# State-space layer: the work between two batches' scans in another order, Softplus as one function, and v of two head pairs at once

## The chip, the cores and the metric

One Trainium2 chip, one of its NeuronCores. The metric is the device time in microseconds (us) from the start of the kernel to its end. TensorE (PE), VectorE (DVE), ScalarE (ACT), GpSimd (POOL) and the DMA queue of SyncE (SP) each run their own list of instructions in order; they wait for each other only through semaphores.

## What is computed

Four transformer-like layers on x of shape 8 x 512 x 256 (batches, positions, features), fp32. Layers 0 and 2 are attention with 16 heads of 16 features, layer 1 is attention with 16 heads of 64 (pairs of heads share 128 columns), layer 3 is a bidirectional state-space (Mamba) layer with a gated MLP. Only layers 1 and 3 are touched. Layer 3, cut to what matters:

```python
def _mamba(h, ...):
    xz = h @ in_proj_W                      # 256 -> 2 x 512
    x, z = jnp.split(xz, 2, axis=-1)
    x = _silu(causal_conv4(x) + conv_b)     # 4 taps
    xdbl = x @ x_proj_W                     # 16 + 32 + 32 columns
    dt = softplus(xdbl[..., :16] @ dt_proj_W + dt_proj_b)
    Bm, Cm = xdbl[..., 16:48], xdbl[..., 48:]
    A = -jnp.exp(A_log)
    def step(hst, inp):                     # over 512 positions
        dA = jnp.exp(dt_t[:, :, None] * A)
        hst = hst * dA + dt_t[:, :, None] * B_t[:, None, :] * x_t[:, :, None]
        y = jnp.einsum('bdn,bn->bd', hst, C_t)
        return (hst, y)
    y = scan(step) + Dp * x
    return y * _silu(z) @ out_proj_W
h = modulate(_ln(x)); fwd = _mamba(h); bwd = flip(_mamba(flip(h)))
x = x + g1 * (fwd + bwd)
h = modulate(_ln(x)); x = x + g2 * (_silu(h @ w1) * (h @ w2) @ w3)
```

In layer 1 the part that matters is `v = h @ Wv` of each head.

## The kernel before

The layers run one after the other; each keeps its weights in SBUF and loops over the 8 batches, with an all-engine barrier after each batch. Nothing is scheduled by a compiler: every engine's list is the order in which the functions below issue instructions.

**Layer 1** (`wide_attention_layer`). `project(pair, which, to)` makes q, k or v of one pair of heads in one PSUM bank, `projected` copies it out on ACT. v is made as 4 position tiles x 2 contraction chunks of matmuls with 128 moving columns (L1016), one v per pair; `values` multiplies the probabilities with it.

**Layer 3** (`mamba_layer`). A batch has two parts.

*The scans.* 2 directions x 16 groups of two states x 4 chunks of 128 channels make 128 units (`UNITS`). For unit i ACT makes two `decay` halves (Exp, L1869) and its share of `dtx_B` (dt·x times B, L1860; 7 instructions for every 4 units on ACT and 1 on POOL, L1797), PE transposes dtx_B into one of two pairs of PSUM banks (`fill_bx`, L1897), DVE runs the recurrence over 2 x 512 positions in one instruction (`scan_unit`, L1827), POOL multiplies the state by C (L1812, tile `hc`) and PE sums it over the states (`y_sum`, L1908). There are three decay buffers, three of h, four of hc. The last `y_sum` of a chunk is added and gated on DVE (`combine_last`, L1837 and L1840).

*Between the scans* (`between_*`). The end of batch b and the start of batch b + 1 are woven together: LayerNorm of the next batch (stats and scaling on DVE, L90 to L101; reciprocal root on POOL, L107 and L110; transposes on PE, L117; scale and shift on ACT into `hT`, L125), input projection in 8 chunks of 128 (`project_in`, L1650; x in the first four, z in the others), `out_proj` of batch b (L1661), the gate rows (L191, L198, L204), 24 convolution taps on DVE (L1530, the first tap on ACT, L1575), Silu (L1591, L1584), x_proj (L1674), dt_proj (L1684), transposes of B (L1697), Softplus, residual and second LayerNorm of batch b, the MLP (L1713, L1634, L1561, L1738), dt·x and its transposes (L1556, L1727, L1624). Softplus is built as max(v, 0) + ln(1 + exp(-|v|)): Abs (L1604), max on DVE (L1543), Exp (L1615), Ln (L1619), an addition on DVE (L1553). SP copies dt to 128 partitions (`dt_rep`, 16 DMAs, L1492) and C to DRAM (L1487), and waits for all of them at the end (L1495). Then comes the barrier, and after it the first 7 scalings `dtx_B`, the first decays and the first fill, before the first scan can start.

Before batch 0 the start half runs alone, after batch 7 the end half alone.

## Time and profile before

| | us |
|---|---|
| median of 3 runs | 6822.93 (6816.15 to 6824.26) |
| the profiled execution | 6823.96 |
| its span, first to last instruction | 6822.1 |
| PE busy | 6011.6 (88%) |
| DVE busy | 4556.8 (67%) |
| ACT busy | 4284.6 (63%) |
| POOL busy | 2641.1 (39%) |

The state-space layer starts at 3662 us and takes the rest, 3160 us. In it one batch repeats every 387.55 us. Times below are on the span's clock. In the rows, a line "start us, us, engine line op" is a run of like instructions; brackets at its end give the idle time before it and what ended it.

### The profile page before, as it was taken

To read this page: it belongs to the slowest core of one execution; us is meant where nothing else is said; L and a number is where in the kernel's file an instruction comes from. 1 tells how busy PE (TensorE), PEld (TensorE's weight loads), DVE (VectorE), ACT (ScalarE), POOL (GpSimd) and SP (SyncE) were. 2 spreads that over 40 slices of the span, in tenths; PEclk is the share of its full clock that TensorE was granted. 3 is DMA by queue.
4 is the path that set the end of the run, shared out by engine and by line. 5 is a ranking of instruction groups with operands and counts; after the bars stand their busy time and mean duration, and the time that the engine had idled before them with its cause. 6 is when DMAs were issued, how large, how long until landed. Compare 5 with 4: busy or idle time off the path is not lost. (4 is left out here: it accounts for less than half of the span.)

```text
span 6822.1 us, 79092 instructions
## 1 busy us (share of the span) xinstructions
PE 6011.6 (88%) x29136; PEld 3143.3 (46%) x29136; DVE 4556.8 (67%) x5015; ACT 4284.6 (63%) x6948; POOL 2641.1 (39%) x1956
## 2 busy tenths in 40 slices
PE   6989987999999996998986898888898888888898
PEld 3444444555555553453443444444444444444444
DVE  4565743344344434566573997979798897979797
ACT  2344434444454542434443988979797998979796
POOL 0000002222222220000000876949495785949496
PEclk8999998999999997999997998989899998989899
DMA  4312211000000002131221101011100201010100
GB/s 108 54 31 52 33 29 39 1 1 1 1 1 1 1 1 53 30 58 32 52 37 41 34 19 52 27 44 30 41 30 15 56 21 51 29 43 29 41 30 19
DMA packets 152081, 216.13 MB, mean 32 GB/s; under 512 B 23649, under 2 KB 90489, under 8 KB 151185
## 3 DMA queue, kind: packets, MB, share of 16 engines
q1 hardware_dynamic: 151552, 211.01, 13.7%
q8 instruction: 233, 3.82, 0.2%
q14 instruction: 152, 1.24, 0.1%
q10 hardware_dynamic: 144, 0.07, 0.0%
HBM read 146.48 MB, written 30.44 MB: 26 GB/s over the span
## 5 line engine op out<-in xcount | busy, mean ns | idle before, releaser
L1827 DVE TENSOR_TENSOR_SCAN l__h<-l__decay,l__psum 128x1024 f32<-128x1024 f32 x1024 | 2278.0, 2272 | 113.0 <-ACT l__decay L1869 90.3
L1812 POOL TENSOR_TENSOR l__hc<-l__h,l__c_rep 128x1024 f32<-128x1024 f32 x1024 | 2039.8, 2003 | 220.6 <-DVE l__h L1827 176.6
L1897 PEld LDWEIGHTS l__psum<-ident,l__dtx_B 128*128 128x128 f32 x8192 | 900.2, 143 | 1151.0 <-DVE l__h L1827 653.4
L1897 PE MATMUL l__psum<-ident,l__dtx_B 128*128 128x128 f32 x8192 | 1142.3, 284 | 305.8 <-ACT l__dtx_B L1860 258.1
L1869 ACT ACTIVATE l__decay<-l__dt_rep,l__a_neg 128x511 f32<-128x511 f32 x2048 | 1355.2, 714 | 2.5 <-DVE l__h L1827 2.4
L1860 ACT ACTIVATE l__dtx_B<-l__dtx_T,l__b_T 128x512 f32<-128x512 f32 x1792 | 1199.7, 715 | 71.9 <-PEq L1922 60.7
L1908 PE MATMUL l__psum<-l__hc,l__gather 128*64 128x512 f32 x4096 | 1111.9, 621 | 18.3 <-POOL l__hc L1812 17.9
L107 POOL TENSOR_SCALAR l__ln_var_eps<-l__ln_mean_var 128x4 f32<-128x4 f32 x64 | 15.2, 237 | 2424.9 <-DVE l__ln_mean_var L93 2424.3
L566 DVE TENSOR_REDUCE l__row_max<-l__psum 128x1 f32<-128x512 f32 x1024 | 657.4, 686 | 249.4 <-PE l__psum L581 248.1
L1055 POOL TENSOR_SCALAR l__probs<-l__probs,l__rec 128x512 f32<-128x512 f32 x512 | 349.5, 696 | 968.4 <-DVE l__rec L1051 968.4
L759 ACT ACTIVATE l__probs<-l__psum 128x1024 f32<-128x1024 f32 x512 | 515.7, 1025 | 282.6 <-PE l__psum L808 278.1
L1041 DVE TENSOR_REDUCE l__neg_max<-l__psum 128x2 f32<-128x1024 f32 x256 | 312.9, 1223 | 437.1 <-PE l__psum L1035 436.3
L581 PE MATMUL l__psum<-l__k_stack,l__q_stack 96*128 96x512 bf16 (+1 forms) x1024 | 418.9, 422 | 137.7 <-PEq L931 87.6
L1181 ACT ACTIVATE l__probs_T<-l__psum 128x512 f32<-128x512 f32 x256 | 152.8, 597 | 446.9 <-PE l__psum L1219 446.9
L1046 ACT ACTIVATE l__probs<-l__psum,l__neg_max 128x512 f32<-128x512 f32 x512 | 346.7, 682 | 44.6 <-DVE l__neg_max L1041 27.1
L808 PE MATMUL l__psum<-l__q_stack,l__k_stack 98*128 98x512 bf16 (+1 forms) x1024 | 333.7, 417 | 8.7 <-ACT l__probs L759 4.4
L1035 PE MATMUL l__psum<-l__kT,l__qT 64*128 64x512 f32 x1024 | 296.3, 656 | 35.4 <-PEq L1324 24.0
L1219 PEld LDWEIGHTS l__psum<-ident,l__probs 128*128 128x128 f32 x2048 | 224.6, 143 | 203.3 <-POOL l__probs L1055 121.0
L1908 PEld LDWEIGHTS l__psum<-l__hc,l__gather 128*64 128x64 f32 x4096 | 203.5, 135 | 207.9 <-issue 168.5
L581 PEld LDWEIGHTS l__psum<-l__k_stack,l__q_stack 96*128 96x128 bf16 (+1 forms) x1024 | 98.8, 98 | 435.1 <-DVE l__row_max L566 291.3
L917 PE MATMUL l__psum<-l__w,l__g 128*128 128x256 f32 x1024 | 278.1, 380 | 12.4 <-ACT l__g L781 12.4
L1219 PE MATMUL l__psum<-ident,l__probs 128*128 128x128 f32 x2048 | 288.4, 284 | 0.6
(169 smaller groups left out, 7042.8 us busy)
## 6 DMA issues: line engine op xcount, KB each, us to landing
l__c_rep<-l__c_dram SPq DMA_DIRECT2D x512, 128.0 KB, 2.8
l__dt_rep<-l__dt SPq DMA_DIRECT2D x128, 256.0 KB, 4.9
l__parts_dram<-l__parts SPq DMA_DIRECT2D x64, 384.0 KB, 4.5
l__q_stack<-l__parts_dram SPq DMA_DIRECT2D x192, 128.0 KB, 6.6
l__k_stack<-l__parts_dram SPq DMA_DIRECT2D x192, 128.0 KB, 9.7
l__w<-in_l_w SPq DMA_DIRECT2D x6, 1024.0 KB, 9.1
mod_w<-in_mod_w SPq DMA_DIRECT2D x2, 2816.0 KB, 12.8
x_sb<-in_x SPq DMA_DIRECT2D x1, 4096.0 KB, 27.4
```

The source lines that it names most:

```text
L566: nc.vector.tensor_reduce(mx[:, h // GH, t, h % GH:h % GH + 1], max_bank(n), AX.X, ALU.max).then_inc(S["max_taken"], 1)
L581: nc.tensor.matmul(max_bank(n), qs[0:k_max, h, t * P:(t + 1) * P], ks[0:k_max, h, :], start=True, stop=True).then_inc(S["max_filled"], 1)
L759: nc.scalar.activation(probs[:, n % SLOTS:n % SLOTS + 2, :], pair(n), ACT.Exp, scale=float(HD) ** -0.5).then_inc(S["exp"], 1)
L1046: nc.scalar.activation(probs[:, u % SLOTS, j, :], bank[QK + 2 * (u % 2) + j], ACT.Exp, bias=neg_max[:, u % SLOTS, j:j + 1], accum_out=sums ...
L1055: nc.gpsimd.tensor_scalar(probs[:, u % SLOTS, j, :], probs[:, u % SLOTS, j, :], rec[:, u % SLOTS, j:j + 1], 1.0, ALU.mult, ALU.mult)\
L1219: last = nc.tensor.transpose(bank[TR + j][:, k * P:(k + 1) * P], probs[:, u % SLOTS, j, k * P:(k + 1) * P], ident[:, :])
L1812: nc.gpsimd.tensor_tensor(hc[:, i % HCS, :, :], h[:, i % HS, :, :], c_of_i, ALU.mult).then_inc(S["hc"], 1)
L1827: nc.vector.tensor_tensor_scan(both(h[:, i % HS, :, :]), both(decay[:, i % DECAYS, :, :]), both(bx_psum(i)), 0.0, ALU.mult, ALU.add).then_ ...
L1860: nc.scalar.activation(dtx_B[:, k % 2, t, :, j, :], dtx_T[:, w, t, :].rearrange("p (b d) -> p b d", d=HB), ACT.Copy, scale=b_T[:, w, t, NJ ...
L1869: nc.scalar.activation(decay[:, i % DECAYS, s, 1:T], dt_rep[:, w, c, s, 1:T], ACT.Exp, scale=a_neg[:, g, c, s:s + 1]).then_inc(S["decay"], 1)
L1897: last = nc.tensor.transpose(bx_psum(i)[:, s, t * P:(t + 1) * P], dtx_B[:, k % 2, t, 2 * c + s, :, :].rearrange("p j d -> p (j d)"), ident ...
L1908: last = nc.tensor.matmul(y_psum[half(s), c, :], gather[:, :], hc[:, i % HCS, s, :], start=(g == 0), stop=(g == GROUPS - 1))
```

## The change

1. Layer 1: v is made for two pairs of heads at once. The PSUM bank that took four position tiles of one pair takes two position tiles of two pairs: 2 tiles x 2 chunks of matmuls with 256 moving columns instead of 4 x 2 with 128. The number of ACT copies stays.
2. Softplus is one ACT function (ACT.Softplus), straight from PSUM; Abs, Exp, Ln, the max and the addition go.
3. The next batch's LayerNorm statistics are taken on DVE after unit 123 of 128, its scaling after unit 125; PE transposes them after unit 126's scan. The four first `project_in` stand around the last `y_sum` in PE's list. ACT's `hT` waits for all 128 hc.
4. dt_proj, B and C of the two directions lie in different rows: direction 0 has dt in rows 0 to 31 and B in 64 to 95, direction 1 has dt in rows 64 to 95 and B in 32 to 63. x_proj goes to banks 6 and 7, and its first chunk stands between two `project_in`.
5. The 7 first scalings on ACT and the one on POOL, the first two decays and the first two fills are issued ahead of the barrier; the scans' waits count from there. dt_rep has a semaphore per chunk, and SP waits only for C at the end.
6. Tiles that live only between the scans are laid out around the new early buffers with gaps; `decay` and `c_rep` swap places.

The core of the diff:

```diff
 (project, layer 1)
-                for t in range(TT):
+                both = slice(pair // 2 * 2 * P, (pair // 2 + 1) * 2 * P)
+                for u in range(2):
+                    t = pair % 2 * 2 + u
                     for c in range(DC):
-                        last = nc.tensor.matmul(to[:, t * P:(t + 1) * P], hT[:, c, t * P:(t + 1) * P], wv[:, c, cols],
+                        last = nc.tensor.matmul(to[:, u * 2 * P:(u + 1) * 2 * P], hT[:, c, t * P:(t + 1) * P],
+                                                wv[:, c, both], start=(c == 0), stop=(c == DC - 1))
 (mamba_layer)
+    FILLED = 2
+    DECAYED = DECAYS - 1
+    STATS_AFTER, SCALED_AFTER = UNITS - 5, UNITS - 3
+    dt_rows = (slice(0, DTL), slice(2 * NS, 2 * NS + DTL))
+    c_rows = (slice(DTL, DTL + NS), slice(0, NS))
+    b_rows = (slice(DTL + NS, DTL + 2 * NS), slice(NS, 2 * NS))
 (between_gpsimd)
+            if begin:
+                pool.wait_ge(S["taps"], 2 * (TAPS - 1) * IC)
+                nc.gpsimd.memset(decay[:, :, :, 0:1], 0.0).then_inc(S["zero"], 1)
+                pool.wait_ge(S["bT"], 1)
+                pool.wait_ge(S["dtxT"], 2 * IC)
...
+                scale_last(0)
 (between_vector)
-            if begin:
-                ahead.stats(nc, dve, nxt, 0)
-            if end:
-                combine_last(0)
-            if begin:
-                ahead.scaled(nc, dve, nxt, 0)
             if end:
-                for c in range(1, IC):
+                for c in range(IC):
                     combine_last(c)
...
-                    nc.vector.tensor_scalar(relu(c), dt_banks(c), dtb[:, c:c + 1], 0.0,
-                                            ALU.add, ALU.max).then_inc(S["relu"], 1)
...
-                    nc.vector.tensor_tensor(dt_all[:, c, :, :], relu(c), dt_all[:, c, :, :], ALU.add).then_inc(S["dt"], 1)
 (between_scalar)
+            def softplus(c):
+                act.wait_ge(S["dt_filled"], c + 1)
+                nc.scalar.activation(dt_all[:, c, :, :], dt_banks(c), ACT.Softplus, bias=dtb[:, c:c + 1])\
+                    .then_inc(S["dt"], 1)
...
+                act.wait_ge(S["c_out"], 32)
+                act.wait_ge(S["dtxT"], 2 * IC)
+                for q in range(IC):
+                    scale_pair(q)
...
+                for i in range(DECAYED):
+                    act.wait_ge(s_dt_rep[split(i)[2]], dt_rep_of(nxt))
+                    decay_unit(i)
 (between_tensor)
+                if c == 3:
+                    pe.wait_ge(S["dt"], 1)
+                for w in range(2):
+                    last = nc.tensor.matmul(dt_banks(c)[:, w, :], dtw[dt_rows[w], c * P:(c + 1) * P],
+                                            dc[dt_rows[w], w, :], start=True, stop=True)
...
+                for i in range(FILLED):
+                    fill_bx(i)
 (the scans, DVE)
+                        if i == STATS_AFTER and begin:
+                            ahead.stats(nc, dve, b + 1, 0)
+                        if i == SCALED_AFTER and begin:
+                            ahead.scaled(nc, dve, b + 1, 0)
 (the scans, ACT)
+                    act.wait_ge(S["hc"], UNITS)
+                    between_scalar(act, True, begin, b + 1)
 (the scans, PE)
+                    if begin:
+                        pe.wait_ge(S["scan"], UNITS - 1)
+                        norm.tensor(nc, pe, 0, bank[0:DC])
                     y_sum(UNITS - 2)
+                    if begin:
+                        pe.wait_ge(S["scan"], UNITS)
+                        pe.wait_ge(S["hT"], DC)
+                        project_in(pe, 0)
+                        project_in(pe, 1)
                     y_sum(UNITS - 1)
+                    if begin:
+                        project_in(pe, 2)
+                        project_in(pe, 3)
```

How the lists stand, in two places. PE at the end of a batch's scans and through the gap, first before (L1908 is y_sum, L1650 the input projection, L1661 the output projection, L1674 x_proj, L1684 dt_proj, L1713 the MLP's first matmuls, L1727 the transposes of dt·x):

```order
L1908 MATMUL l__psum<-l__hc,l__gather 64x512 x8
L117 MATMUL l__psum<-ident,l__ln_xn 128x128 x8
L1650 MATMUL l__psum<-l__hT,l__win 128x512 x8
L1661 MATMUL l__psum<-l__wout,l__silu_z 128x256 x16
L198 MATMUL l__psum<-l__gate_diag,ones 128x256 x2
L1650 MATMUL l__psum<-l__hT,l__win 128x512 x8
L1674 MATMUL l__psum<-l__xs,l__xproj 96x512 x8
L1684 MATMUL l__psum<-l__dt_and_c,l__dtw 128x512 x4
L1697 MATMUL l__psum<-ident,l__dt_and_c 128x32 x8
L1684 MATMUL l__psum<-l__dt_and_c,l__dtw 128x512 x4
```

and now PE at the same place (L1975 is y_sum, L1710 the input projection, L1719 the output projection, L1731 x_proj):

```order
L1975 MATMUL l__psum<-l__hc,l__gather 64x512 x4
L117 MATMUL l__psum<-ident,l__ln_xn 128x128 x8
L1975 MATMUL l__psum<-l__hc,l__gather 64x512 x2
L1710 MATMUL l__psum<-l__hT,l__win 128x512 x4
L1975 MATMUL l__psum<-l__hc,l__gather 64x512 x2
L1710 MATMUL l__psum<-l__hT,l__win 128x512 x4
L1719 MATMUL l__psum<-l__wout,l__silu_z 128x256 x16
L198 MATMUL l__psum<-l__gate_diag,ones 128x256 x2
L1710 MATMUL l__psum<-l__hT,l__win 128x512 x4
L1731 MATMUL l__psum<-l__xs,l__xproj 96x512 x2
L1710 MATMUL l__psum<-l__hT,l__win 128x512 x4
L1731 MATMUL l__psum<-l__xs,l__xproj 96x512 x6
```

The last y_sum, unit 127's, now stands behind two chunks of the input projection; before, all sums stood ahead of it.

ACT from x_proj's result to the next batch's scans, before (L1594 takes it from PSUM, L1860 are the scalings, L1869 the decays; the two branches are the barrier):

```order
L1594 ACTIVATE l__dt_and_c<-l__psum 96x512 x2
L1599 ACTIVATE l__y<-l__xs,l__dp 128x512 x4
L1604 ACTIVATE l__dt<-l__psum,l__dtb 128x1024 x2
L1608 ACTIVATE l__b_T<-l__psum 128x256
L1604 ACTIVATE l__dt<-l__psum,l__dtb 128x1024 x2
L125 ACTIVATE l__hT_mlp<-l__psum,l__cur 128x512 x2
L1615 ACT_TABLE_LOAD
L1615 ACTIVATE l__dt<-l__dt 128x1024 x4
L1619 ACT_TABLE_LOAD
L1619 ACTIVATE l__dt<-l__dt 128x1024 x4
L1624 ACTIVATE l__dtx_T<-l__psum 128x4x128 x4
L1634 ACT_TABLE_LOAD
```

and now (L1677 takes x_proj's result, L1649 is Softplus, L1661 the MLP's Silu, L1505 the scalings, L1520 the decays; rows up to the barrier):

```order
L1677 ACTIVATE l__dt_and_c<-l__psum 96x512 x2
L1649 ACT_TABLE_LOAD
L1649 ACTIVATE l__dt<-l__psum,l__dtb 128x1024 x2
L1681 ACTIVATE l__b_T<-l__psum 128x256
L1649 ACTIVATE l__dt<-l__psum,l__dtb 128x1024 x2
L125 ACTIVATE l__hT_mlp<-l__psum,l__cur 128x512 x2
L1655 ACTIVATE l__dtx_T<-l__psum 128x4x128 x2
L1661 ACT_TABLE_LOAD
L1661 ACTIVATE l__hid<-l__psum 128x512
L1655 ACTIVATE l__dtx_T<-l__psum 128x4x128 x6
L1505 ACTIVATE l__dtx_B<-l__dtx_T,l__b_T 128x8x64 x7
L1661 ACTIVATE l__hid<-l__psum 128x512 x2
```

Behind them an ACT_TABLE_LOAD and four decays (L1520) stand ahead of the barrier too. Five table loads a batch become four; the four instructions of y_first (L1599 before) stand ahead of x_proj's result.

## Rows read from the trace of the kernel before

**Rows 1.** The profile page, part 1: busy time and share of the span by engine.

```profile
PE 6011.6 (88%) x29136; PEld 3143.3 (46%) x29136; DVE 4556.8 (67%) x5015; ACT 4284.6 (63%) x6948; POOL 2641.1 (39%) x1956
```

**Rows 2.** Stretches: length, then busy us (instructions) by engine, granted clock, DMA.

```profile
4065.80:4071.00 5.20, 5.20 (x8) 2.39 (x9) 1.78 (x6) 1.28 (x2) 0.00 (x0) 0.62 0.00 0
...
4101.00:4112.70 11.70, 10.86 (x19) 4.26 (x17) 5.36 (x5) 5.45 (x7) 0.00 (x0) 0.50 0.00 0
...
4151.10:4446.00 294.90, 264.34 (x1521) 135.18 (x1519) 287.70 (x137) 288.44 (x471) 272.73 (x158) 0.99 0.09 28
```

**Rows 3.** Timeline, batch 0's last scans and the restart behind the barrier.

```profile
4046.45 11.00 DVE L1827 TENSOR_TENSOR_SCAN l__h<-l__decay,l__psum 128x1024 f32<-128x1024 f32 x5 [0.16 <-ACT l__decay L1869]
...
4057.60 2.00 POOL L1812 TENSOR_TENSOR l__hc<-l__h,l__c_rep 128x1024 f32<-128x1024 f32 x1 [0.18 <-DVE l__h L1827]
...
4143.94 4.39 ACT L1860 ACTIVATE l__dtx_B<-l__dtx_T,l__b_T 128x512 f32<-128x512 f32 x7 [9.21 <-PEq L1922]
...
4148.35 1.28 ACT L1869 ACT_TABLE_LOAD   x1
...
4151.11 4.46 DVE L1827 TENSOR_TENSOR_SCAN l__h<-l__decay,l__psum 128x1024 f32<-128x1024 f32 x2 [6.98 <-ACT l__decay L1869]
```

**Rows 4.** Timeline, the gap's first 14 us: next LayerNorm, projection, first tap.

```profile
4057.43 1.40 DVE L90 BATCH_NORM_STATS2 l__ln_stats<-x_sb 128x6 f32<-128x256 f32 x4
...
4058.86 0.38 DVE L93 BATCH_NORM_AGGREGATE l__ln_mean_var<-l__ln_stats 128x2 f32<-128x6 f32 x4
...
4060.00 1.43 POOL L110 TENSOR_TENSOR l__ln_rstd<-l__ln_var_eps,minus_half 128x4 f32<-128x4 f32 x1
...
4061.47 1.38 DVE L101 TENSOR_SCALAR l__ln_xn<-x_sb,l__ln_mean_var,l__ln_rstd 128x256 f32<-128x256 f32 x4 [0.93 <-POOL l__ln_rstd L110]
...
4064.21 1.54 ACT L125 ACTIVATE l__hT<-l__psum,l__cur_ahead 128x512 f32<-128x512 f32 x2 [11.92 <-PE l__psum L117]
...
4069.69 0.60 ACT L1571 ACTIVATE l__x_padded<-l__psum 128x512 f32<-128x512 f32 x1 [3.94 <-PE l__psum L1650]
...
4071.24 15.99 DVE L1530 SCALAR_TENSOR_TENSOR l__xs<-l__x_padded,l__conv_w,l__xs 128x512 f32<-128x512 f32 x24 [3.62 <-ACT l__xs L1575]
```

**Rows 5.** Timeline, x_proj to the last Abs of Softplus.

```profile
4090.19 7.11 PE L1674 MATMUL l__psum<-l__xs,l__xproj 128*96 128x512 f32 x16 [0.69 <-ACT l__silu_z L1584]
...
4097.34 0.59 ACT L1594 ACTIVATE l__dt_and_c<-l__psum 96x512 f32<-96x512 f32 x1 [0.27 <-PE l__psum L1674]
4097.83 2.54 ACT L1599 ACTIVATE l__y<-l__xs,l__dp 128x512 f32<-128x512 f32 x4
...
4099.81 0.61 PE L1697 MATMUL l__psum<-ident,l__dt_and_c 32*128 32x32 f32 x7
...
4110.05 1.11 ACT L1604 ACTIVATE l__dt<-l__psum,l__dtb 128x1024 f32<-128x1024 f32 x1 [2.30 <-PE l__psum L1684]
```

**Rows 6.** Timeline, MLP, Ln and the end of the gap.

```profile
4112.78 12.90 PE L1713 MATMUL l__psum<-l__hT_mlp,l__w 128*128 128x512 f32 x24 [0.87 <-ACT l__hT_mlp L125]
...
4119.24 3.90 ACT L1619 ACTIVATE l__dt<-l__dt 128x1024 f32<-128x1024 f32 x4
...
4133.90 7.37 PE L1738 MATMUL l__psum<-l__w,l__hid 128*128 128x256 f32 x24
...
4142.03 0.69 DVE L222 TENSOR_TENSOR x_sb<-x_sb,l__res_tmp 128x512 f32<-128x512 f32 x1
```

**Rows 7.** Timeline, the same MLP matmuls behind batch 7.

```profile
6810.72 5.45 PE L1738 MATMUL l__psum<-l__w,l__hid 128*128 128x256 f32 x24 [1.41 <-DVE l__hid L1561]
```

**Rows 8.** Timeline, the start half alone: dt's copies, and ACT behind the barrier.

```profile
3734.88 16.20 SPq L1492 DMA_DIRECT2D l__dt_rep<-l__dt  x16
...
3756.39 4.39 ACT L1860 ACTIVATE l__dtx_B<-l__dtx_T,l__b_T 128x512 f32<-128x512 f32 x7 [11.25 <-PEq L1766]
```

**Rows 9.** Timeline, PE in layer 1: one v projection and what follows it.

```profile
1243.73 1.95 PE L1016 MATMUL l__psum<-l__wv,l__hT 128*128 128x128 f32 x16
1245.52 1.04 PE L117 MATMUL l__psum<-ident,l__ln_xn 128*128 128x128 f32 x8
```

More of the change, by code:

```diff
@@ L1027, in projected @@
             else:
[L1028 removed]
+                half = slice(pair % 2 * 2, pair % 2 * 2 + 2)
+                nc.scalar.activation(v[:, pair // 2 % 2, half, :].rearrange("p t n -> p (t n)"), of, ACT.Copy)\
                     .then_inc(S["proj"], 1)
@@ new lines, in silu_x, with y_first @@
+            def silu_x(c):
+                for w in range(2):
+                    act.wait_ge(S["taps"], 2 * ((TAPS - 1) * c + TAPS - 2) + w + 1)
+                    nc.scalar.activation(xs[:, c, w, :], xs[:, c, w, :], ACT.Silu).then_inc(S["xs"], 1)
+            def y_first(c):
+                act.wait_ge(S["xs"], 2 * (c + 1))
+                if end:
+                    act.wait_ge(S["gated"], c + 1)
+                nc.scalar.activation(y[:, c, :], xs[:, c, 0, :], ACT.Copy,
+                                     scale=dp[:, c:c + 1]).then_inc(S["y_first"], 1)
@@ L1628, in between_scalar @@
+            if end:
+                norm.scalar(nc, act, 1 if begin else 0, bank[6:8], hT_mlp, cur, scale2, shift2)
             if begin:
                 take_dtx_T(0)
-                take_dtx_T(1)
             if end:
-                for j in range(HC):
-                    act.wait_ge(S["up_filled"], j + 1)
-                    nc.scalar.activation(hid[:, j, :], bank[UP_BANKS[j][0]], ACT.Silu).then_inc(S["silu"], 1)
+                silu_up(0)
             if begin:
-                take_dtx_T(2)
@@ L1864, in decay_unit, with decays @@
[L1864 to L1865 removed]
+                            act.wait_ge(S["bx_filled"], IC * (k - 1) - FILLED)
+                        scale_pair(q)
+                    def decays(i):
                         if i >= DECAYS:
                             act.wait_ge(S["scan"], i - DECAYS + 1)
[L1868 to L1870 removed]
```

427 lines of the change are left out of this document (224 added, 203 removed).

## The prediction

> **What bounds the kernel now.** I read the page's busy times first [rows 1]: PE is busy 88% of the span, which says nothing on the state-space layer, where one batch repeats every 387.55 us (ACT's first scaling at 3756.39 and at 4143.94) [rows 3, 8]. So I cut one batch into two stretches and read each.
>
> In the **scans** (4151.1 to 4446.0) ACT is busy 288.44 of 294.90 us, DVE 287.70, PE 264.34 at clock 0.99 [rows 2]. ACT sets the pace: up to unit 123 DVE still waits for a decay, and from there it runs five scans in 11.00 us, 2.20 each, on its own [rows 3]. ACT issued 225 scalings and 248 decay halves, 473 instructions, and one table load (1.28) between the barrier at 3756.39 and scan 123 at 4046.45: 290.06 us, so (290.06 - 1.28) / 473 = 0.6105 us each [rows 3, 8]. DVE alone would have needed about 124 x 2.20 + 3 = 276.
>
> In the **gap** nothing is full. Take t = 0 at the end of the last scan, 4046.45 + 11.00 = 4057.45 [rows 3]. Then: hT ready at 8.3, input projection from there at clock 0.62, first tap of DVE at 13.8, taps done at 29.8 [rows 2, 4]; x_proj 32.7 to 39.9, its result out at 40.5, last Abs done at 53.7 with PE at clock 0.50, Ln from 61.8 to 65.7, MLP's last matmul 83.8, last residual 85.3, barrier released 86.5, first scan 93.7 [rows 2, 3, 5, 6]. It is a chain from engine to engine, and the sum is a new chain.
>
> **The scans, part by part.** Seven scalings, one load and four decay halves leave the stretch behind the barrier: 11 x 0.6105 + 1.28 = 8.0 us less, since ACT sets the pace from barrier to unit 123. Their cover in the gap: between the transposes of dt·x and the MLP's second and third Silu, ACT waits for PE anyway (below). The statistics and the scaling of the next batch enter DVE's list after unit 123 and 125, where DVE is alone on the path: 0.15 (copy) + 1.40 + 0.38, less overlaps, 1.85, plus 1.38 [rows 4] = 3.3 us more. POOL's root (1.43, [rows 4]) has two scans of time, 4.4 us, beside one product of 2.0: no wait. Net -4.7 us for batches 0 to 6, -8.0 for batch 7, which has no next one: 7 x 4.7 + 8.0 = **-40.9**.
>
> **The gap's head.** Now LayerNorm's chain (8.3 us) is gone, but hT waits for the last product hc: POOL works 4057.60 to 4059.60 [rows 3], so hT starts at 2.25 and takes 1.54 [rows 4]: 3.8. PE then starts the input projection, 4.5 us earlier than before. This is not what DVE gets. The sum of unit 127 stands behind two chunks of the projection, and `combine_last(3)` and the gate diagonals stand ahead of the taps on DVE. From hT to the first chunk before was 3.95 us (4065.75 to 4069.69, [rows 4]; low clock, [rows 2]), the second chunk 1.7 more, the sum 1.1: 3.8 + 5.65 + 1.15 = 10.6. Then 1.33 for the combination and 0.9 for the gates: taps from 13.0, against 13.8 before. Without that wait they could start at 3.8 + 3.95 + 1.55 = 9.3. So of 4.5 us the path keeps 0.8, and the gap's head as a whole costs 3.3 in the scans for it. Taps 15.99: done at **29.0**.
>
> **x_proj and dt.** Silu of z and x alternate, and three quarters of x_proj no longer wait for all of z. Output projection from 14.0 (32 matmuls of 256 columns, 6.9 by 5.45 / 24 less the tail, [rows 7]), gates 1.0, gate rows 22.6, table load to 23.9; then 0.55 a Silu (0.60 for the like copy, [rows 4], less its overlap with the next); the fourth chunk's input projection pair ends at 30.4, silu of chunk 2 at 32.1, three y_first (2.54 / 4 = 0.63 each, [rows 5]) at 34.0, silu of chunk 3 at 35.1. Last x_proj pieces 35.15 to 36.9, second copy out 37.7 (before 40.5): 2.8 us won, against 3.6 had y_first(0..2) not stood ahead. Softplus' table load runs to 39.0 while PE makes dt.
>
> dt_proj of the two directions lies in row strips 0 and 64. The trace has the like: transposes out of rows 64 to 95 start at 4099.81, in the middle of dt_proj out of rows 0 to 31, which runs on to 4110 [rows 5]. I take it that the strips overlap, so four matmuls take three slots, then two per step. Slots are 0.43 at the high clock; in this stretch the clock was 0.50 from about 3 us after its start [rows 2], and then they are 0.85. dt ready at 39.4, 40.2, 43.9, 45.6 (one by one, as before, the last would be at 37.7 + 12.1 = 49.8). I price Softplus like Abs, Exp and Ln of the same 1024 columns, 1.11 alone and 3.90 for four [rows 5, 6]: done at 40.5, 41.5, 45.0, 46.7. The trace shows no Softplus; the lower bound is that row, the upper is open and is the rival below.
>
> By the Trainium skill, "TensorE: Matmul & The Clock Gate", Part 3: matmuls in different row groups run at the same time; by that rule the forecast stands, against it the serial rival. By "ScalarE activation tables: per-element evaluation and per-set limits", section "What a function is on this engine", the price of an ACTIVATE does not depend on the function and a change of set costs 1283 ns; the table loads agree (1.28), no run yet shows Softplus.
>
> **MLP and end.** LayerNorm 2 is long ready (xn at 36.4). Its transposes 47.0, hT_mlp 48.3, first transposes of dt·x 48.6, first up projection at low clock (0.85 a matmul for the first 5 us, which is how 24 of them took 12.90 before instead of 10.5, [rows 6]) to 54.4. Then three rounds of transposes and copies, 1.4 each, to 59.2; ACT's seven scalings, 4.39, to 63.6, while PE makes the other two up projections, 58.3 to 65.2. Silu and product 66.7. Down projection: 5.45 where PE had idled 1.4 us and stayed at the high clock [rows 7], 7.37 where it had not [rows 6]; 5.3 here, to 72.0. Residual 73.5; the two early fills on PE to 73.9 (now the last work, 1.9 us, 3.7 at low clock); barrier 1.2 [rows 3, 6]: release at **75.2**, with ACT's load and four decays done at 70. dt's copies: first issue 40.5, the eighth by 48.6, and 5.3 us to land (3751.08 to 3756.4, [rows 8]): 54, before ACT needs them at 67. Against 86.5: -11.3 a gap, x 7 = **-79.1**.
>
> **The start half alone.** Before, dt's first copy went at 3734.88, the last 16.2 later, and the barrier waited for it: 3756.39 [rows 8]. Now: taps end 3704.9, x_proj out 3708.7, Softplus 3711.6 to 3716.9, transposes 3720.8, scalings 3725.2, load 1.28, decays 2.56, barrier 1.2: 3730.3, so **-26**.
>
> **Small terms.** v in layer 1: 16 matmuls of 128 columns take 1245.52 - 1243.73 = 1.79 us [rows 9]; 8 of 256 take 5.45 / 24 x 8 = 1.82 by the MLP's row with its tail, 1.71 without [rows 7]: up to 0.08 x 64 = **-5**, between 0 and -8 where PE is not what is waited for. The layer's weights: two more DMAs behind a memset of the whole x_proj tile: **+1.5**.
>
> **Sum:** -40.9 - 79.1 - 26 - 5 + 1.5 = -149.5, from 6823.96 (this execution; the median is 6822.93): 6674. I say **6674 us**.
>
> **Rivals.**
> *The clock stays high.* x_proj, dt and the up projection follow more closely; if 0.85 never appears, dt comes 2 us earlier, the first up projection 2.6: release at 70.5, 7 x 4.7 = 33 us less: 6641. Against it: PE fell to 0.50 in just this work of 32 rows [rows 2].
> *Row strips don't overlap.* dt's last 4.2 us later, in 8 places: +34, 6708. With the fills at low clock (+1.8 x 7) 6720.
> *Softplus is dear (the other side).* Four a batch stand on the path, 8 batches. They cancel the gain at 149.5 / 32 = 4.7 us more each, 5.8 in all; at 7 us each the time is 6674 + 32 x 5.9 = 6863. For it: no row has the function. Against it: all four functions in the rows cost the same.
> *It doesn't do what it says.* If the barrier still waited for something, it would be dt's copies: their last lands at 41 + 16.2 + 5.3 = 62, before 75. So no.
>
> **How the numbers follow.** Forecast (6650 to 6700) 0.58; clock high (below 6650) 0.17; strips serial or more low clock (6700 to 6730) 0.17; worse but faster still 0.05; Softplus dear, or the scans slowed, beyond 6838: 0.03. A gap's release is uncertain by 3 us, 21 in all, the scans by 0.5 a batch. The range 6630 to 6722 leaves out 0.2. Faster by over 0.2% (14 us, about what a measurement tells from no change) 0.96, within 0.01, slower 0.03.
>
> **What would show it.** Batch period 371.5 us: last scan 296.4 behind the barrier, release 75 behind it. DVE idle from about 4 to 10.7 us in the gap, ended by y_sum; first tap at 13.0; Softplus 1.1 us each; first scan within 0.1 us of the barrier. Wrong if Softplus is longer, if the scans' period is no longer 15 ACT instructions in 9.16 us, or if fills or copies end the gap later than 77.

## The result, and the profile of the changed kernel

The changed kernel takes **6622.64 us** (median of 4 runs, 6619.90 to 6629.14) where the kernel before takes 6819.68 (4 runs): ratio 0.9713, 95% interval 0.9700 to 0.9725. The forecast was 6674, with a range of 6630 to 6722. The direction was right, the size too small by some 50 us: the time lies below the range.

The profiled execution of the changed kernel took 6629.14 us, its span 6627.4. First the page's busy times (they answer to [rows 1]). Then two rows of the changed kernel that cut the span: the first weight DMA of the state-space layer, and the group of all 1024 scans of DVE (shortest, median and longest ns, then the start of the first and of the last). The pair behind them is the same from the kernel before.

```profile
PE 5888.8 (89%) x28624; PEld 3055.1 (46%) x28624; DVE 4491.2 (68%) x4951; ACT 4212.2 (64%) x6876; POOL 2643.4 (40%) x1956
```

```profile
3642.19 0.41 SPq L1466 DMA_DIRECT2D l__win<-in_l_win  x1
...
L1904 DVE TENSOR_TENSOR_SCAN l__h<-l__decay,l__psum x1024: 2251/2261/2290, 3714.8 to 6571.4; 128x1024 f32<-128x1024 f32 x171
```

```profile
3662.56 0.41 SPq L1453 DMA_DIRECT2D l__win<-in_l_win  x1
...
L1827 DVE TENSOR_TENSOR_SCAN l__h<-l__decay,l__psum x1024: 2258/2262/2290, 3763.6 to 6767.2; 128x1024 f32<-128x1024 f32 x171
```

Cut there, the 194.7 us between the spans fall apart as follows. The forecast is put into the same cuts: the 7.2 us between barrier and first scan [rows 3] count to the start, so -26 + 1.5 - 7.1 there.

| stretch | before | changed | difference | forecast |
|---|---|---|---|---|
| layers 0 to 2 | 3662.56 | 3642.19 | -20.4 | -5 |
| layer 3 up to the first scan | 101.0 | 72.6 | -28.4 | -31.6 |
| first scan to last scan | 3003.6 | 2856.6 | -147.0 | -112.9 |
| last scan to the end | 54.9 | 56.0 | +1.1 | 0 |

Two terms carry the miss: the batches (34 us) and the layers ahead (15 us). The batches first. This is the gap behind batch 0 in the changed kernel, from its timeline (start, length, engine, line, operation, what ended the idle time before); t = 0 is the end of the last scan, 4007.96 + 4.45 = 4012.41. It answers to [rows 3 to 6].

```profile
4007.96 4.45 DVE L1904 TENSOR_TENSOR_SCAN l__h<-l__decay,l__psum 128x1024 f32<-128x1024 f32 x2
4012.55 2.00 POOL L1888 TENSOR_TENSOR l__hc<-l__h,l__c_rep 128x1024 f32<-128x1024 f32 x1 [0.18 <-DVE l__h L1904]
4014.64 1.45 ACT L125 ACTIVATE l__hT<-l__psum,l__cur_ahead 128x512 f32<-128x512 f32 x2 [10.37 <-POOL l__hc L1888]
4016.23 6.56 PE L1710 MATMUL l__psum<-l__hT,l__win 128*128 128x512 f32 x8 [1.83 <-ACT l__hT L125]
4022.72 1.08 PE L1975 MATMUL l__psum<-l__hc,l__gather 128*64 128x512 f32 x4
4023.85 0.69 DVE L1914 TENSOR_TENSOR l__y<-l__psum,l__y 128x512 f32<-128x512 f32 x1 [6.09 <-PE l__psum L1975]
4050.37 0.59 ACT L1677 ACTIVATE l__dt_and_c<-l__psum 96x512 f32<-96x512 f32 x1 [0.27 <-PE l__psum L1731]
4051.02 1.99 PE L1745 MATMUL l__psum<-l__dt_and_c,l__dtw 32*128 32x512 f32 x8 [0.68 <-ACT l__dt_and_c L1677]
4053.40 1.62 PE L1745 MATMUL l__psum<-l__dt_and_c,l__dtw 32*128 32x512 f32 x6
4054.55 2.13 ACT L1649 ACTIVATE l__dt<-l__psum,l__dtb 128x1024 f32<-128x1024 f32 x2
4058.07 3.70 PE L1768 MATMUL l__psum<-l__hT_mlp,l__w 128*128 128x512 f32 x8 [1.16 <-ACT l__hT_mlp L125]
4066.29 4.39 ACT L1505 ACTIVATE l__dtx_B<-l__dtx_T,l__b_T 128x512 f32<-128x512 f32 x7
4073.79 5.45 PE L1807 MATMUL l__psum<-l__w,l__hid 128*128 128x256 f32 x24 [1.41 <-DVE l__hid L1612]
4079.07 1.91 PE L1527 MATMUL l__psum<-ident,l__dtx_B 128*128 128x128 f32 x16
4080.00 0.69 DVE L222 TENSOR_TENSOR x_sb<-x_sb,l__res_tmp 128x512 f32<-128x512 f32 x1
4082.02 2.29 DVE L1904 TENSOR_TENSOR_SCAN l__h<-l__decay,l__psum 128x1024 f32<-128x1024 f32 x1 [1.33 <-PEq L1999]
```

And four stretches of the same gap: length, busy time (instructions) of PE, of its weight loads, DVE, ACT and POOL, then the granted clock and the DMA's share and GB/s. They answer to [rows 2].

```profile
4016.00:4020.00 4.00, 3.77 (x5) 1.72 (x6) 1.72 (x3) 0.08 (x1) 0.00 (x0) 0.50 0.00 0
4020.00:4035.00 15.00, 15.00 (x52) 9.42 (x52) 11.12 (x20) 8.35 (x12) 0.00 (x0) 0.93 0.00 1
4051.00:4055.00 4.00, 3.98 (x25) 2.03 (x25) 1.97 (x3) 3.99 (x5) 0.00 (x0) 1.00 0.20 48
4058.00:4062.00 4.00, 3.92 (x12) 1.97 (x13) 0.07 (x1) 2.47 (x5) 0.00 (x0) 1.00 0.97 254
```

Step by step, us after the last scan:

| step | forecast | measured |
|---|---|---|
| hT ready | 3.8 | 3.7 |
| DVE's wait for the last sum ends | 10.6 | 11.4 |
| x_proj's second copy out | 37.7 | 38.55 |
| last dt_proj matmul | 45.6 | 42.6 |
| last Softplus | 46.7 | 44.3 |
| first up projection done | 54.4 | 49.4 |
| down projection done | 72.0 | 66.8 |
| barrier released | 75.2 | 69.6 |

Up to x_proj the chain ran as written, 0.9 us late. The difference comes in one stretch, between x_proj and the first up projection, where the forecast had PE at half clock (0.85 us a matmul) and the rows have it at 1.00: 10.8 us instead of 16.7. The rest of the chain only carries it on.

### The profile page after: what moved, and what is told of

Same layout as the page of the kernel before. It is cut to its first block and busy times, and to the rows that moved or that the text cites. A ratio compares the mean times of both kernels' runs of the same rounds, so it can differ in the third digit from the quotient of the medians.

```text
span 6627.4 us, 77923 instructions
## 1 busy us (share of the span) xinstructions
PE 5888.8 (89%) x28624; PEld 3055.1 (46%) x28624; DVE 4491.2 (68%) x4951; ACT 4212.2 (64%) x6876; POOL 2643.4 (40%) x1956
## 5 line engine op out<-in xcount | busy, mean ns | idle before, releaser
L1520 ACT ACTIVATE l__decay<-l__dt_rep,l__a_neg 128x511 f32<-128x511 f32 x2048 | 1350.9, 710 | 14.9 <-DVE l__h L1904 14.8
L1505 ACT ACTIVATE l__dtx_B<-l__dtx_T,l__b_T 128x512 f32<-128x512 f32 x1792 | 1195.4, 710 | 38.4 <-PEq L1999 36.1
L1975 PE MATMUL l__psum<-l__hc,l__gather 128*64 128x512 f32 x4096 | 1115.5, 623 | 12.4 <-POOL l__hc L1888 12.0
L1975 PEld LDWEIGHTS l__psum<-l__hc,l__gather 128*64 128x64 f32 x4096 | 203.9, 135 | 198.1 <-issue 171.8
```

The lines of the kernel that those rows point to most:

```text
L1505: nc.scalar.activation(dtx_B[:, k % 2, t, :, j, :], dtx_T[:, w, t, :].rearrange("p (b d) -> p b d", d=HB), ACT.Copy, scale=b_T[:, w, t, NJ ...
L1520: nc.scalar.activation(decay[:, i % DECAYS, s, 1:T], dt_rep[:, w, c, s, 1:T], ACT.Exp, scale=a_neg[:, g, c, s:s + 1]).then_inc(S["decay"], 1)
L1975: last = nc.tensor.matmul(y_psum[half(s), c, :], gather[:, :], hc[:, i % HCS, s, :], start=(g == 0), stop=(g == GROUPS - 1))
```

## The experiments

All share one measure besides the median: the time from the first to the last scan in the profiled execution, which holds seven batch periods and not the layers ahead, whose length differs from one execution to the next (the first scan began at 3714.8 us in the changed kernel and at 3701.4 in norm_back and ysum_first, whose work up to there is the same). It is 3003.6 before and 2856.6 in the changed kernel.

### dt_proj: does the clock depend on the rows?

```diff
# strips_one, from the changed kernel
-    dt_rows = (slice(0, DTL), slice(2 * NS, 2 * NS + DTL))
+    dt_rows = (slice(0, DTL), slice(0, DTL))
...            # c_rows, b_rows, x_cols: both directions as direction 0
# strips_96: besides
-   last = nc.tensor.matmul(dt_banks(c)[:, w, :], dtw[dt_rows[w], c * P:(c + 1) * P],
-                           dc[dt_rows[w], w, :], start=True, stop=True)
+   last = nc.tensor.matmul(dt_banks(c)[:, w, :], dtw[:, c * P:(c + 1) * P],
+                           dc[:, w, :], start=True, stop=True)
```

**strips_one.** 

> The changed kernel with both directions of dt_proj in rows 0 to 31, as before the change (16 matmuls one after the other). Theory A, the short dt stretch is what kept PE at its high clock: serial, the clock falls some 3 us after its start as in the kernel before, dt's last matmuls take 0.85 to 0.9 us each, the transposes and the first up projection behind them run low too: 6 to 9 us more per gap, 7 gaps, and 3 to 6 in the start half: 6665 to 6690. Rival B, the clock stays high for another reason (the work ahead of dt is closer packed): only the matmuls that no longer overlap count, 16 x 0.43 = 6.9 instead of 4.0 us, 8 times: about +23, 6646. Rival C, dt is hidden behind Softplus: within 8 us of the changed kernel.

**strips_96.** 

> As strips_one, but the 16 matmuls read all 96 rows of the tile (the weights of the 64 other rows are zero), so that the same columns run on three times the rows. Theory A, it is the 32-row work that lets the clock fall: clock 1.00 through dt, 16 x 0.43 = 6.9 us instead of 4.0, about +23 us: 6646, some 30 below strips_one. Rival: the clock falls here too, because of the idle times around dt or the time since the gap began: the same time as strips_one, 6665 to 6690.

**before_96**, the second edit in the kernel before (its `dtw` tile becomes `[ROWS, DI]`, zero below the first rows). 

> The kernel before with dt_proj over all 96 rows of the tile (weights of the other 64 rows zero): the same 16 matmuls and columns, more rows. Theory, the 32-row stretch costs the clock: clock near 1.00 from dt to the up projection, dt in 7.6 instead of 12.0 us, transposes of the LayerNorm 0.9 and up projection 2.4 us less: -7.7 a gap, 7 gaps, and 2 to 4 in the start half: 6820 - 56 = 6764. Rival: the clock falls for what lies ahead (idle times around x_proj): no change, 6813 to 6825.

| kernel | median | ratio to before (95%) | first to last scan |
|---|---|---|---|
| strips_one | 6672.85 | 0.9786 (0.9772 to 0.9801) | 2902.3 |
| strips_96 | 6649.66 | 0.9753 (0.9739 to 0.9768) | 2880.3 |
| before_96 | 6785.66 | 0.9949 (0.9934 to 0.9964) | 2973.8 |

The groups of dt_proj's 128 matmuls over the whole layer, in the order before, before_96, changed, strips_one, strips_96 (shortest, median and longest ns of one, first and last start):

```profile
L1684 PE MATMUL l__psum<-l__dt_and_c,l__dtw x128: 587/1052/1217, 3713.1 to 6433.5; 32*128 32x512 f32 x128
```

```profile
L1684 PE MATMUL l__psum<-l__dt_and_c,l__dtw x128: 592/593/697, 3706.4 to 6395.6; 96*128 96x512 f32 x128
```

```profile
L1745 PE MATMUL l__psum<-l__dt_and_c,l__dtw x128: 587/587/692, 3694.2 to 6252.6; 32*128 32x512 f32 x128
```

```profile
L1745 PE MATMUL l__psum<-l__dt_and_c,l__dtw x128: 587/588/1056, 3688.2 to 6296.6; 32*128 32x512 f32 x128
```

```profile
L1745 PE MATMUL l__psum<-l__dt_and_c,l__dtw x128: 592/592/697, 3679.8 to 6264.5; 96*128 96x512 f32 x128
```

A matmul of 512 columns shows 0.59 us at the high level (2.4 GHz, granted clock 1.00) and 1.05 and more at the low one (1.2 GHz, 0.50). Serial over 32 rows (before, strips_one) part of them are at 1.05 or above; over 96 rows, with the same columns and the same order, none is, in either kernel, in any of the 8 places; with the two directions in strips none is either. So the low clock of [rows 2] belongs to the serial 32-row stretch. In the changed kernel the strips avoid it: the stretch is 4.0 us instead of 9 to 12. Whether it is the shorter stretch that spares the clock, or that two strips work at a time (64 rows instead of 32), no run separates. Shortness alone is no safe reason: in strips_one the first slow matmul began 1.8 to 4.8 us behind the start of the stretch. In the changed kernel the strips are worth 45.7 / 7 = 6.5 us a batch, of which 23.7 / 7 = 3.4 is the matmuls' overlap and 3.1 the clock. That strips run side by side is plain from the rows above: 8 matmuls in 1.99 us. (By the Trainium skill, "TensorE: Matmul & The Clock Gate", Part 3: matmuls in different row groups run at the same time; the trace agrees with that rule.)

before_96 gave 29.8 / 7 = 4.3 us a gap where 7.7 were expected. Up to the last residual the clock brought more: behind batch 0 it was done 79.0 us after the last scan instead of 85.3, 6.3 earlier. The rest was lost at the barrier, which also waits for dt's copies to 128 partitions, and these start only behind Ln and DVE's addition. Three rows of before_96 (its last scan of batch 0 ends at 4047.96): the 16 copies, the last residual, and ACT's first work behind the barrier.

```profile
4108.22 16.32 SPq L1492 DMA_DIRECT2D l__dt_rep<-l__dt  x16
4126.24 0.69 DVE L222 TENSOR_TENSOR x_sb<-x_sb,l__res_tmp 128x512 f32<-128x512 f32 x1
4130.15 4.39 ACT L1860 ACTIVATE l__dtx_B<-l__dtx_T,l__b_T 128x512 f32<-128x512 f32 x7 [10.38 <-PEq L1922]
```

The last copy is issued at 4123.4, and a copy takes 4.8 us to land (median of the 16, 5.9 at most). The residual is done at 4126.93, the barrier opens 3.2 us later; before it was 1.2 us [rows 3, 6]. PE's wait ahead of the dt·x transposes is not the place, though the expectation of before_both below takes it for that. Here is this group in the kernel before and in before_96 (idle time of PE ahead of it, by what ended it):

```profile
L1727 PE MATMUL l__psum<-ident,l__xs 128*128 128x128 f32 x256 | 42.3, 320 | 37.4 <-ACT l__dtx_T L1624 24.4 <-DVE l__xs L1556 13.0
```

```profile
L1727 PE MATMUL l__psum<-ident,l__xs 128*128 128x128 f32 x256 | 43.3, 325 | 38.9 <-DVE l__xs L1556 29.4 <-ACT l__dtx_T L1624 9.6
```

DVE ends more of the wait than before, 29.4 us instead of 13.0, but ACT ends less, and the sum over the 8 places grew only from 37.4 to 38.9.

### Softplus: alone, and with the clock

```diff
# before_softplus, from the kernel before
-   nc.scalar.activation(dt_all[:, c, :, :], dt_banks(c), ACT.Abs, bias=dtb[:, c:c + 1]).then_inc(S["abs"], 1)
+   nc.scalar.activation(dt_all[:, c, :, :], dt_banks(c), ACT.Softplus, bias=dtb[:, c:c + 1]).then_inc(S["dt"], 1)
...            # ACT's Exp and Ln, DVE's relu and addition go
```

**before_softplus.** 

> The kernel before with Softplus in one ACT instruction in the place of Abs, Exp, Ln and DVE's two additions, nothing else. Theory: in a gap Exp and Ln with their loads (10.4 us) lie beside the up projection, which runs 12.9 us at partly low clock, so PE is not waiting for them and Softplus gives 0 to 2 us a gap; in the start half there is no up projection, and the last of dt comes 10 to 12 us earlier: 6819 - 12 - 7 = 6800. Rival: the dt chain is the path in the gap as well: 6 us and more a gap, 6765.

**before_both.** 

> before_softplus together with dt_proj over all 96 rows (before_96, 6786, alone -33). In before_96 PE waited 3.5 us a gap for DVE's additions behind Ln, so that half of what the clock gave was lost to the chain; with Softplus this wait goes. Theory, the two hide each other: together more than the sum of the parts by 3 us a gap, 6819 - 33 - 19 - 21 = 6746. Rival, they add up: 6767.

before_softplus: 6803.37 us, ratio 0.9977 (0.9967 to 0.9986), first to last scan 3004.1. before_both: 6742.66 us, ratio 0.9893 (0.9876 to 0.9910), first to last scan 2943.2. Softplus alone gives **nothing** between the scans (3004.1 against 3003.6), and all it gives lies in the start half: the first scan stands 84.0 us behind the first weight DMA instead of 101.0. Together with the clock the two give 60.4 / 7 = 8.6 us a gap, against 4.3 + 0. The theory held: each hid behind the other, Exp and Ln behind an up projection at low clock, and a part of the clock's gain behind Ln and the copies that follow it (behind batch 0 the copies start 45.3 us after the last scan in before_both, 60.3 in before_96). A Softplus itself took what Abs took: in the gap above two in 2.13 us.

### The first scalings, decays and fills

```diff
# late_first, from the changed kernel
-    FILLED = 2
-    DECAYED = DECAYS - 1
+    FILLED = 0
+    DECAYED = 0
...            # scale_pair, scale_last, decay_unit and fill_bx leave the gap, and open the scans
```

> The changed kernel with the first seven scalings, POOL's, the first two decays and the first two fills back behind the barrier, as before. Theory: these 11 ACT instructions and one table load (8.0 us) stand again in the stretch that ACT paces, while the gap ends only when the two fills are off PE (1.9 us less, of which the residual gives back some 0.3): +6.3 us in each of 8 batches: 6623 + 50 = 6673. Rival: DVE or POOL paces the scans by now (POOL's four products and a scaling take 8.7 of 9.17 us), so ACT's 8.0 us are partly slack: +2 us a batch, 6639.

6689.73 us, ratio 0.9809 (0.9794 to 0.9823); first to last scan 2919.0: 62.4 / 7 = **8.9 us** a batch. Of this 8.2 lie between the barrier's release and the last scan (7.2 to the first scan, then 298.7 instead of 297.6); the prediction's own term, 8.0, stood. My expectation had 6.3, since it let the gap end 1.9 us earlier without the fills. Behind batch 0 it ends only 0.4 earlier (release 69.2 us after the last scan instead of 69.6): in the rows of the gap above the residual is done at 4080.69, the fills at 4080.98. Over the seven gaps it ends 0.7 later, because in four of the changed kernel's gaps PE was back at the high clock sooner in the input projection (first two chunks in 5.1 to 5.4 us instead of 6.5), and in none of late_first's. The rival, slack of ACT among the scans, is out.

### The next LayerNorm among the last scans, and the order at the gap's head

```diff
# norm_back, from the changed kernel (PE's transposes move behind the sum of unit 126)
-    STATS_AFTER, SCALED_AFTER = UNITS - 5, UNITS - 3
+    STATS_AFTER, SCALED_AFTER = UNITS - 1, UNITS - 1
# ysum_first
-   project_in(pe, 0)
-   project_in(pe, 1)
    y_sum(UNITS - 1)
+   project_in(pe, 0)
+   project_in(pe, 1)
# norm_on_act: ahead.scaled leaves DVE; DVE makes -mean * rstd behind scan 125, ACT behind its last decay:
+   nc.scalar.activation(norm.xn[:, t, :], ahead.of(b + 1)[:, t, :], ACT.Identity,
+                        bias=norm.mv[:, 0, t, 0:1], scale=norm.rs[:, 0, t:t + 1])
```

**norm_back.** 

> The changed kernel with the next batch's statistics and scaling behind the last scan in DVE's list (POOL's root behind the last product). Theory: the last scans shrink by what the two took there (1.85 and 3.04, the second beside POOL's product), and hT comes at about 8.5 instead of 3.7 us after the last scan; all that follows moves with it: net within 1 us a gap, 6616 to 6630. Rival: the LayerNorm among the scans was worth the whole gain that the gap's head shows: +4.8 us a gap, 6656.

**ysum_first.** 

> The changed kernel with the last sum of C times h ahead of the first two chunks of the input projection on PE. Theory: in the gap DVE idles 6.1 us for that sum and its taps begin 13.6 us after the last scan; with the sum first DVE waits for x_padded and the first tap instead, taps from about 9.7. The output projection, gate rows and all behind them move with it: -3.5 to -4 us per gap, 7 gaps: 6595 to 6599. Rival: the chain behind the gates is held by the chunks of the input projection (z) and by ACT, whose order does not change: the gain is under 1.5 us a gap, 6612 to 6622.

**norm_on_act.** 

> The changed kernel with the scaling of the next batch's LayerNorm on ACT, which is idle after its last decay, instead of DVE, where it took 3.04 us between two scans; one small operation on DVE (0.15 us) makes the shift. Theory: the last scans are DVE's alone, so 2.9 us a gap: 6623 - 20 = 6603. Rival: POOL's root and products are then late (2.0 us each against 2.2 a scan), hT waits for the last one: under 1.5 us a gap, 6613 to 6623.

| kernel | median | ratio to before (95%) | first to last scan |
|---|---|---|---|
| norm_back | 6613.15 | 0.9696 (0.9680 to 0.9712) | 2847.9 |
| ysum_first | 6603.35 | 0.9686 (0.9670 to 0.9702) | 2840.4 |
| norm_on_act | 6596.66 | 0.9668 (0.9654 to 0.9682) | 2828.5 |

norm_back: this part of the change is worth less than nothing, the kernel is 8.7 / 7 = 1.2 us a batch faster without it. From the first scan of a batch to its last it takes 292.9 us instead of 297.6, and the gap behind it 72.4 instead of 68.9 (mean of seven): the scans pay 4.7 for the 3.5 that the gap wins. Three rows show why the price is above the 3.3 of the forecast. Changed kernel, DVE's four subtractions and POOL's product at the same time:

```profile
4004.99 3.04 DVE L101 TENSOR_SCALAR l__ln_xn<-x_sb,l__ln_mean_var,l__ln_rstd 128x256 f32<-128x256 f32 x4
...
4005.22 2.01 POOL L1888 TENSOR_TENSOR l__hc<-l__h,l__c_rep 128x1024 f32<-128x1024 f32 x1 [0.15 <-DVE l__h L1904]
```

norm_back, the same four with POOL at rest but for two memsets of 0.11 us:

```profile
3997.94 1.38 DVE L101 TENSOR_SCALAR l__ln_xn<-x_sb,l__ln_mean_var,l__ln_rstd 128x256 f32<-128x256 f32 x4 [1.83 <-POOL l__ln_rstd L110]
```

DVE stands still for most of POOL's product and takes 3.04 us for 1.38 of work. The forecast used the 1.38 of [rows 4], read where POOL was idle. On ACT, which is idle there, the same work took 2.08 us off the path:

```profile
4006.65 2.08 ACT L1960 ACTIVATE l__ln_xn<-x_sb,l__ln_mean_var,l__ln_rstd 128x256 f32<-128x256 f32 x4 [2.06 <-PE l__psum L1527]
```

norm_on_act won 28.1 / 7 = 4.0 us a batch where 2.9 were expected. The scans gave just these 2.9 (294.7 us instead of 297.6); the rest came from the gap, where PE did its normalisation's transposes later, idled less and began the input projection at the high clock (first two chunks 3.67 us instead of 6.56 behind batch 0, and 3.67 in four of the seven gaps).

ysum_first won 2.3 us a gap of the 3.5 expected. DVE's wait of 6.09 went, and its taps began at 9.0 instead of 13.6, but the path is PE's list: the gate rows came 20.3 instead of 22.8 us after the last scan, since the projection's four chunks stand ahead of the output projection either way. The theory had the size by the taps, which are not last there.

### Layer 1: why the clock held

```diff
# v_alone: the kernel before with the v projection of two pairs (the change's first part)
# old_v_pad, new_v_pad: the kernel before, and v_alone, with one matmul of no use ahead of each v projection
+   nc.tensor.matmul(to[:, 0:P], hT[:, 0, 0:P], wv[:, 0, cols], start=True, stop=True)
```

**v_alone.** 

> The kernel before with only the v projection of two pairs. Clock theory: in layer 1 of the kernel before, PE's clock fell at each batch boundary (first 5 us of a batch at 0.52), in the changed kernel it does not from the third boundary on, although the idle time ahead is the same 3.42 us; the narrower matmuls saved 0.06 us x 64 only. So v alone gives about -20 us (6800), and layer 1's windows around the boundaries read clock 1.00. Rival, v is worth its matmuls only and the clock came from something else in the changed kernel: -4 to -5 us (6815), boundaries at 0.97 as before.

**old_v_pad.** 

> The kernel before with one more 128-column matmul ahead of each of the 8 v projections of a pair (its product is overwritten): work that does nothing. Theory, timing: whether PE's clock falls after the 3.42 us of idle at a batch boundary of layer 1 depends on when the boundary falls, not on v's form, so 0.9 us more work a batch can end the low clock: -23 + 7 = -16 us against before (about 6802), boundaries at 1.00. Rival: it hangs on v's form (128 against 256 columns): the boundaries stay at 0.97 and the time is 7 us longer, 6825.

**new_v_pad.** 

> v_alone (6795) with the same overwritten 128-column matmul ahead of each v projection as in old_v_pad, 0.9 us a batch. If v's form decides over the clock behind the batch boundaries of layer 1: they stay at 1.00, 6795 + 7 = 6802. If it is the time at which the boundaries fall: they can be low again, 6802 + 15 to 23 = 6817 to 6825.

| kernel | median | ratio to before (95%) | seven batches of layer 1 |
|---|---|---|---|
| before | 6817 to 6820 | 1 | 1360.8 |
| v_alone | 6794.59 | 0.9969 (0.9956 to 0.9983) | 1339.8 |
| old_v_pad | 6828.51 | 1.0013 (1.0004 to 1.0023) | 1368.8 |
| new_v_pad | 6820.01 | 1.0000 (0.9990 to 1.0010) | 1362.6 |

(Last column: first to last copy of the batch's modulation into `cur`.) The same boundary of two batches, kernel before:

```profile
1653.49 14.08 PE L1318 MATMUL l__psum<-l__w,l__g 128*128 128x256 f32 x64
1671.00 2.08 PE L1035 MATMUL l__psum<-l__kT,l__qT 64*128 64x512 f32 x4 [3.42 <-PEq L1324]
```

and changed kernel:

```profile
1651.12 14.08 PE L1321 MATMUL l__psum<-l__w,l__g 128*128 128x256 f32 x64
1668.62 1.13 PE L1038 MATMUL l__psum<-l__kT,l__qT 64*128 64x512 f32 x4 [3.42 <-PEq L1327]
```

The work and the idle time ahead are the same 14.08 and 3.42 us; in the one the clock has fallen behind them (2.08 us for four matmuls), in the other not (1.13). v_alone brings the gain by itself, and it is gone again in new_v_pad, which has v's new form and 0.9 us more work a batch: 1362.6 where 1339.8 + 7 x 0.9 = 1346 would be the work. old_v_pad, where I had expected the pad to bring the clock back, came out where its rival had put it: at every boundary the clock fell at once or within 5 us (granted 0.50 to 0.66 on the mean of these 5 us). So neither v's new form nor the 0.9 us keeps the clock by itself. What remains is when the boundaries fall, and executions of one and the same layer 1 show it. before_both changes nothing in that layer, and its v has the old form. Two of its boundaries:

```profile
1277.36 1.13 PE L1035 MATMUL l__psum<-l__kT,l__qT 64*128 64x512 f32 x4 [3.43 <-PEq L1324]
```

```profile
1662.30 2.08 PE L1035 MATMUL l__psum<-l__kT,l__qT 64*128 64x512 f32 x4 [3.43 <-PEq L1324]
```

At the first and the second boundary (1277.4 and 1469.0 us) PE kept its clock, from 1662.3 on it did not; in the kernel before, with the same instructions, it lost it at all seven. The new form shows the same: norm_back and ysum_first kept it at all seven and took 1339.7 and 1339.8 us, the profiled execution of the changed kernel and strips_one lost it at the first two and took 1344.9 and 1345.0, norm_on_act at three. So the moment decides, with the work unchanged; which moments keep the clock, these runs do not say. Where the clock holds, a boundary follows the last by 191.6 us in the old form and by 191.1 or 191.2 in the new, so that v's work is worth 0.5 us a batch, and each fall costs 2.8 or 2.9 more. The new form does not secure the clock, but it goes with it: seven of the ten profiled executions that have it without a pad kept the clock at every boundary, and of the four with the old form three lost it at every one.

### A version that beats both

```diff
# head, from norm_on_act
+   # ACT's wait for the last product stands behind hT instead of ahead of it
+   # ACT's normalisation waits for the fills of the ring's older slot only
    project_in(pe, 0)
-   project_in(pe, 1)
    y_sum(UNITS - 1)
+   project_in(pe, 1)
# all_four, from head
+   # y_first(0..2) behind silu_x(3); fill_bx(0) ahead of the down projection
-   DECAYED = DECAYS - 1
+   DECAYED = DECAYS
-   PAIRS_AHEAD = 6
+   PAIRS_AHEAD = 7
```

**head.** 

> norm_on_act (6597) with hT no longer waiting for the last product, its inputs made as soon as the ring's slot is free, and the last sum of C times h on PE behind the first chunk of the input projection instead of the second. hT should stand 0.6 to 1.0 us after the last scan instead of 3.7, the output projection start at 9.5 to 10 instead of 12.0: 2 us a gap, 14 in all: 6583. Rival: DVE's last two products beside POOL's hold the last gate, so that the output projection doesn't start before 11: 6590 or more.

**all_four.** 

> head with the y_first copies behind the last Silu of x (0.9 us a gap where PE waited for it), a third decay unit in the gap (2 ACT instructions, 1.2 us, out of the stretch that ACT paces, 8 times), and the first fill of the ring ahead of the down projection (0.3 us a gap, up to the residual): 6.3 + 9.8 + 2 = 18 us less than head, 6565. Rival: the ring of three decays is then full and ACT waits for scans in every unit: the scans' period grows over 9.17 us per four, 2 us a batch and more, 6590.

head: **6566.73 us**, ratio 0.9628 (0.9614 to 0.9642), first to last scan 2806.4. all_four: **6550.68 us**, ratio 0.9607 (0.9593 to 0.9621), first to last scan 2792.1: 72 us under the changed kernel. In head hT stood 1.0 us after the last scan and the output projection began at 9.3 instead of 12.0; the gain between first and last scan is 22.1 / 7 = 3.2 us a gap, above the 2 expected. In all_four 14.3 us more went there, of 18 expected, and the third decay unit did not slow the scans, but they won only 0.6 us a batch by it (294.1 us on the mean instead of 294.7) where 1.2 were expected. And here the clock is not safe any more: the longest of the 128 dt_proj matmuls took 1056 ns in head and in all_four, 692 in the changed kernel. It fell in two of the eight places in head and in one in all_four, and such a gap was 1.9 us longer. PE in all_four's gap behind batch 0:

```profile
4029.80 3.11 PE L1748 MATMUL l__psum<-l__dt_and_c,l__dtw 32*128 32x512 f32 x6
4032.85 1.97 PE L117 MATMUL l__psum<-ident,l__ln_xn 128*128 128x128 f32 x8
```

The same six matmuls take 1.62 us in the changed kernel, the transposes 1.09. In all_four x_proj runs without its 0.91 us of idle time, but head still has it and lost the clock too, while its other six places, with the same work, kept it; the strips are the same in all. Why it fell in these places is open. Strips make the fall rarer (8 of 8 places in strips_one, none in the changed kernel), they do not exclude it.

## Why the prediction missed, point by point

- **dt and the up projection** (forecast: dt ready at 45.6, first up projection at 54.4): this is the step that failed. I took the clock of 0.50 in [rows 2] as a property of this place and applied it to a stretch that the change had made a third as long. strips_one, strips_96 and before_96 show that it belonged to 16 serial matmuls of 32 rows: in the changed kernel PE stayed at 1.00, dt_proj was done at 42.6 and the first up projection at 49.4. Priced with high clock the gap came out at 70.5 in my own rival; 69.6 were measured. 5.6 us x 7 is 39 of the missing 45 (the layers ahead add 15; scans, start and end take 13 back; the rest is that the gaps were 68.9 on the mean, the first 69.6). The chance of 0.17 for that rival was too low: its counter-evidence was the very work that the change shortened.
- **v in layer 1** (forecast -5, bounds 0 and -8): as work it was right, 0.06 us x 64. The term was -16 in this execution and -21 in v_alone, since the clock behind the batch boundaries comes and goes with the moment at which they fall. The forecast had no term for that clock. Mis-sized, and the range with it: some 4 of the 16 are the work, the rest is the clock, and how much of it an execution gets is luck. norm_back, with the same work up to there, issued its first weight DMA at 3632.1 where the changed kernel did at 3642.2; 5 of these 10 us are that clock.
- **Scans** (forecast -4.7 a batch): ACT's part held (8.2 measured in late_first against 8.0). DVE's part was mis-sized, 4.7 instead of 3.3, since the subtractions took 3.04 instead of 1.38 beside POOL. So the stretch from release to last scan took 297.7 instead of 296.4: +1.3 x 7 the other way, which by luck made the miss of the sum smaller.
- **The gap's head** (forecast: hT at 3.8, the wait for the last sum until 10.6, "of 4.5 us the path keeps 0.8"): right in its order, measured 3.7 and 11.4; the first two chunks behind batch 0 ran at 0.50, not 0.62. That this part of the change costs about what it brings was right in sign, and norm_back puts a number on it: 1.2 us a batch lost.
- **Softplus** (1.11 us by the row of Abs): right to 0.05. The Trainium skill's rule that an ACTIVATE's price does not depend on the function ("ScalarE activation tables: per-element evaluation and per-set limits", "What a function is on this engine") has now its run: two Softplus of 1024 columns in 2.12 and 2.13 us, and the rival at 5.8 is out.
- **Strips overlap**: right, 8 matmuls of 512 columns in 1.99 us; the rival is out.
- **The start half** (-26): measured -21.3 with the weights (barrier at 72.55 us from the first DMA instead of 93.8; forecast -24.5 for both). Of the difference of 3.2 us no run shows the place.
- **The end of the gap**: the fills are last by 0.3 us, as forecast by order, and cost nearly nothing.

The parts for one batch, from the runs: clock and Softplus together 8.6 us, the overlap of the strips 3.4, the first scalings, decays and fills 8.9, the LayerNorm among the scans -1.2. They sum to 19.7 of the 21.0 measured (147.0 / 7). They were taken in different kernels, and parts can cover each other, so the sum is a check and no proof. The rest, 1.3, has no run of its own; x_proj no longer waiting for all of z was forecast at 2.8, and behind batch 0 x_proj's result came 1.9 earlier (38.55 instead of 40.5).

## What to carry to other kernels

A low clock in a trace is a result of the work around it, and here also of the moment: before it is carried into a forecast, ask whether the change shortens or thins exactly that stretch, and give the other level its own line in the sum. Two costs that cover each other show as little or nothing when either is removed alone (Softplus: 0 us a gap; the clock: 4.3; both: 8.6), so take them out together before calling one worthless. When a wait ends early and the time does not follow, look at everything that the barrier waits for: in before_96 it was the copies' landing. A duration of DVE read beside an idle POOL is not its duration beside a busy one.
